# Graph and attention layer: one-hots compared with digits in PSUM, six tiles made in exchange gaps, histogram between parts of a projection, smaller table parts

## The reference

```python
def gnn(x, W, src, dst):                 # 6250 nodes of 256, 100000 edges
    h = x @ W
    mask = (src != dst)
    deg = segment_sum([mask, ones], [dst, loops])
    w = rsqrt(deg)[fsrc] * rsqrt(deg)[fdst] * [mask, ones]
    return segment_sum(w[:, None] * h[fdst], fsrc)
xn = layernorm(x)
x = x + gnn(xn, W, src, dst) + linear_attention(xn)      # 8 heads, elu + 1 features
x = x + top2_moe(layernorm(x))                           # 8 experts, 256 -> 1024 -> 256, gelu
```

## Time and profile before

| | us |
|---|---|
| median of 3 runs | 2474.34 (2472.77 to 2475.92) |
| the profiled execution's own time | 2474.63 |
| its span in the trace | 2472.7 |
| busy: PE, POOL, DVE, ACT | 2159.0, 1382.8, 1166.6, 1148.6 |
| first scatter, last scatter, first gather start at | 250.65, 448.89, 494.04 |

### The profile page before, as it was taken

How to read it: one execution, slowest core, us unless ns; L and a number is a source line. 1 busy time by engine, 2 the same in 40 slices (tenths; PEclk the granted TensorE clock), 3 DMA queues, 4 the chain that set the end, 5 groups by cost and what they waited for, 6 DMA issues and landing times.

```text
span 2472.7 us, 50507 instructions
## 1 busy us (share of the span) xinstructions
PE 2159.0 (87%) x11910; PEld 1729.7 (70%) x11911; DVE 1166.6 (47%) x2173; ACT 1148.6 (46%) x2813; POOL 1382.8 (56%) x1357
## 2 busy tenths in 40 slices
PE   2996897588889999999999887757999999999998
PEld 1664775366766666666666665426999999999997
DVE  8885653156665666656666565463222222222221
ACT  3664114266666666666666665652232323232322
POOL 3420787277777777777777776002454545444443
PEclk9998667799999999999999999957999999999999
DMA  4002000333333333333333337366666666666663
GB/s 147 1 9 43 3 4 3 119 104 104 105 105 105 106 104 105 105 105 105 104 106 104 105 105 101 109 207 195 186 175 187 175 186 178 183 181 180 183 178 79
DMA packets 136249, 289.74 MB, mean 117 GB/s; under 512 B 28580, under 2 KB 77920, under 8 KB 136067
## 3 DMA queue, kind: packets, MB, share of 16 engines
q0 software_dynamic: 67552, 137.24, 23.4%
q1 hardware_dynamic: 68643, 151.89, 19.0%
HBM read 251.51 MB, written 34.37 MB: 116 GB/s over the span
## 4 chain that ended last, share of the span: by engine, by line
PE 50%; POOL 13%; issue 11%; DVE 10%; DVEq 10%; DMA 3%; SPq 1%; ACT 0%; POOLq 0%; ACTq 0%
PE B L1584 15%; PE B L1593 15%; PE B L1480 13%; POOL BIG L507 7%; POOL edge_rows L496 6%; DVE ACC L553 4%; DVEq L884 3%; DVEq L713 2%; DVEq L876 2%; PE B L1553 2%; DMA BIG<-table,W2A 1%; DVE W2A L553 1%; PE B L1453 1%; DVE BIG L553 1%; PE B L1572 1%
## 5 line engine op out<-in xcount | busy, mean ns | idle before, releaser
L507 POOL DMA_INDIRECT BIG<-table,W2A x832 | 787.4, 946 | 297.4 <-issue 225.5
L553 DVE TENSOR_TENSOR ACC<-ACC,B 128x512 f32 x832 | 572.3, 688 | 403.5 <-PE B L1480 294.0
L1157 ACT ACTIVATE BIG<-B,SMALL 128x128 f32<-128x128 f32 (+1 forms) x889 | 251.1, 388 | 532.1 <-PE B L1584 532.0
L1480 PE MATMUL B<-BIG,W2A 128*128 128x256 f32 x1664 | 410.1, 390 | 75.7 <-DVE ACC L553 48.7
L1480 PE MATMUL B<-BIG 128*128 128x256 f32 x1664 | 406.2, 388 | 49.2 <-DMA BIG<-table,W2A 27.0
L1480 PEld LDWEIGHTS B<-BIG,W2A 128*128 128x128 f32 x1664 | 286.3, 189 | 176.3 <-issue 149.0
L1584 PEld LDWEIGHTS B<-BIG,W1A 128*128 128x128 f32 x3360 | 396.7, 194 | 6.7 <-DVE BIG L556 1.4
L1480 PEld LDWEIGHTS B<-BIG 128*128 128x128 f32 x1664 | 293.9, 190 | 153.2 <-issue 114.9
L1584 PE MATMUL B<-BIG,W1A 128*128 128x128 f32 x3360 | 397.4, 277 | 1.0 <-DVE BIG L556 1.0
L1593 PE MATMUL B<-W2A,BIG 128*128 x1680 | 380.1, 379 | 0.7 <-DVE BIG L553 0.7
L527 POOL DMA_INDIRECT out_dram<-BIG,SMALL x105 | 170.7, 1626 | 343.9 <-DVE BIG L556 343.9
(11 more groups left out here) (245 smaller groups left out, 2045.2 us busy)
## 6 DMA issues: line engine op xcount, KB each, us to landing
W1A<-in_w SPq DMA_DIRECT2D x105, 1024.0 KB
BIG<-table,W2A POOLq DMA_INDIRECT x832
W2A<-in_w SPq DMA_DIRECT2D x1, 8192.0 KB, 27.2
token_x<-BIG SPq DMA_DIRECT2D x24, 256.0 KB, 2.1
out_dram<-ACC SPq DMA_DIRECT2D x1, 6144.0 KB
W2A<-in_x SPq DMA_DIRECT2D x1, 3584.0 KB, 13.1
table<-ACC SPq DMA_DIRECT2D x2, 1792.0 KB, 10.2
W2A<-in_x SPq DMA_DIRECT2D x1, 2560.0 KB
```

What stands on the lines that cost most here:

```text
L507: pool.indirect_dma_start(G[h][:, u, :], None, table, bass.IndirectOffsetOnAxis(ap=dst_T[:, c:c + 1], axis=0)).then_inc(gath[h][u // 2], 16)
L553: return dve.tensor_tensor(o, a, b, op)
L1157: return nc.scalar.activation(o, i, fn, **kw)
L1480: last = mm(B[u][:, k * D:(k + 1) * D], OH[h % 2][:, u, k * P:(k + 1) * P], G[h][:, u, :], start=True, stop=True)
```

## The change

Seven edits, all in the preparation of the graph:

1. `digits` is no longer a bfloat16 array in SBUF. `iota` is copied once into PSUM bank B7, and `onehots` compares the digits in SBUF with that bank, spread over 16.
2. The one-hots of tiles 0 to 5 are made inside `compare_lanes`, one in each exchange gap, after `swap_ready` and ahead of the wait for the exchanged keys. Tile k there waits, as everywhere, for the histogram of tile k-2.
3. On PE those six histograms stand behind the projections 24, 28, 30, 34, 35 and 36. The other 43 stand, four to a projection, behind each of its four parts, in the projections 37 to 47. Projection 48 and then both `unpacked_columns` follow.
4. Half of the exchange transfers, and `raw3`, start from POOL instead of SP.
5. The wait for `counts_ready` and the product that follows it stand behind three projections instead of four, and the next such point behind four instead of six.
6. The table parts are 7, 14, 14, 11 and 3 tiles (before 14, 14, 12, 6 and 3), four ahead of the unpacking and the last behind its first four instructions.
7. ACT takes the root of the degrees behind projection 47 instead of 39.

```diff
-HT = 32
-HG = 8
-HIST_END = HT + NT // HG
-PARTS = ((0, 14), (14, 28), (28, 40), (40, 46), (46, NT))
+HT = 37
+HG = 4
+EARLY = (24, 28, 30, 34, 35, 36)
+HIST_END = HT + (NT - 1 - len(EARLY)) // HG
+PARTS = ((0, 7), (7, 21), (21, 35), (35, 46), (46, NT))
...
+            for k, apart in enumerate(SWAPS):
+                pool.wait_ge(swap_ready, k + 1)
+                for p in range(0, P, 2 * apart):
+                    pool.dma_start(swapped[p + apart:p + 2 * apart, :], keys[SWAP_FROM[k]][p:p + apart, :]).then_inc(swap_in_2, 16)
             pool.wait_ge(stage_ready, 1)
...
+            pool.wait_ge(scat, 16 * NROWS)
+            pool.dma_start(raw3, edge_rows[0:CPAD * RPC, :].rearrange("(j p a) r -> p j (a r)", p=P, a=RPC)).then_inc(raw_in, 16)
             pool.wait_ge(kv_done, NT)
...
-                tt(oh_lo[s], digits, lo, ALU.is_equal)
-                tt(oh_hi[s], digits[:, 0:NT, :], hi, ALU.is_equal).then_inc(oh_ready, 1)
+                digits = B[7][:, 0:P].unsqueeze(2)
+                tt(oh_lo[s], lo.to_broadcast([P, P, HB]), digits.to_broadcast([P, P, HB]), ALU.is_equal)
+                tt(oh_hi[s], hi.to_broadcast([P, NT, HB]), digits[:, 0:NT, :].to_broadcast([P, NT, HB]), ALU.is_equal).then_inc(oh_ready, 1)
...
                 dve.sem_inc(swap_ready, 1)
-                dve.wait_ge(swap_in, 16 * sum(P // a for a in SWAPS[0:k + 1]))
+                onehots(k, k % 2)
+                for there in (swap_in, swap_in_2):
+                    dve.wait_ge(there, 16 * sum(P // (2 * a) for a in SWAPS[0:k + 1]))
...
-            for t in range(4):
+            for t in range(3):
                 project(t, t % 2)
             pe.wait_ge(counts_ready, 1)
...
+            def project(t, s, degrees=()):
+                counts = iter(degrees)
                 keys_values(t, s)
+                count_next(counts)
                 features_queries(t, s)
+                count_next(counts)
                 if not isinstance(t, int) or t + 1 < NT:
                     transpose_x(t + 1, 1 - s)
+                count_next(counts)
                 sum_kv(t)
+                count_next(counts)
...
+            for t in range(EARLY[0] // 2 * 2, HT):
                 project(t, t % 2)
-                for k in range(HG):
-                    histogram((t - HT) * HG + k, k % 2)
-            project(HIST_END, HIST_END % 2)
-            histogram(NT - 1, 0)
+                if t in EARLY:
+                    histogram(EARLY.index(t), EARLY.index(t) % 2)
+            for t in range(HT, HIST_END + 1):
+                first = len(EARLY) + (t - HT) * HG
+                project(t, t % 2, range(first, min(first + HG, NT)))
```

More of the change, by code:

```diff
@@ L41 @@
 KEYS = 1024
+LB = LANES.bit_length() - 1
+FILLS = ROW // LANES
 RPC = P // ROW
@@ L78 @@
 SWAP_FROM = (1, 0, 1, 0, 1, 0)
[L79 to L80 removed]
+assert len(EARLY) == len(SWAPS) and HG == 4 and HIST_END < NT - 1 and CT_DVE % 7 == 0
+assert KEYS >= EC + FILLS * NGR and CPAD * RPC >= NROWS * P and 4 * P >= NBK * (RPC - 1)
 assert NGR <= 32 and UNROLL * 5 < 24
@@ L588, in _ @@
             ch.sync()
-            for k in range(3):
-                ch.add(ts(bit_I[:, k:k + 1], p_I, 4 + k, ALU.logical_shift_right, 1, ALU.bitwise_and))
+            for k in range(LB):
+                ch.add(ts(bit_I[:, k:k + 1], p_I, LISTS.bit_length() - 1 + k, ALU.logical_shift_right, 1, ALU.bitwise_and))
             ch.add(ts(list_ofI, list_ofI, LISTS - 1, ALU.bitwise_and))
             ch.sync()
-            for k, sg in enumerate((sg0, sg1, sg2)):
+            for k, sg in enumerate((sg0, sg1, sg2)[0:LB]):
                 ch.add(ts(sg, bit_I[:, k:k + 1], -2.0, ALU.mult, 1.0, ALU.add))
@@ L683, in _ @@
             dve.sem_inc(counts_ready, 1)
-            ch.add(ts(need[:, 0:NGR], need[:, 0:NGR], lane, ALU.is_gt))
+            for k in range(FILLS):
+                ch.add(ts(fill[:, NGR * k:NGR * (k + 1)], need[:, 0:NGR], -float(LANES * k), ALU.add, lane, ALU.is_gt))
             ch.add(ts(t0[:, 0:NGR], iota[:, 0:NGR], -1.0, ALU.mult, float(NGR), ALU.add))
-            ch.add(dve.memset(fill[:, NGR:KEYS - EC], float(NGR)))
+            ch.add(dve.memset(fill[:, FILLS * NGR:KEYS - EC], float(NGR)))
             ch.sync()
-            ch.link(tt(need[:, 0:NGR], need[:, 0:NGR], t0[:, 0:NGR], ALU.mult))
-            ch.link(ts(fill[:, 0:NGR], need[:, 0:NGR], -1.0, ALU.mult, float(NGR), ALU.add))
+            for k in range(FILLS):
+                ch.add(tt(fill[:, NGR * k:NGR * (k + 1)], fill[:, NGR * k:NGR * (k + 1)], t0[:, 0:NGR], ALU.mult))
+            ch.sync()
+            ch.link(ts(fill[:, 0:FILLS * NGR], fill[:, 0:FILLS * NGR], -1.0, ALU.mult, float(NGR), ALU.add))
             ch.link(ts(keysI[0][:, EC:KEYS], fill, float(GN * ((1 << CODE) + 1)), ALU.mult))
@@ L779, in _ @@
             dve.sem_inc(cgroup_ready, 1)
-            with dve.Fori(1, NT // 2) as i:
+            for t in range(len(EARLY), (len(EARLY) + 1) // 2 * 2):
+                onehots(t, t % 2)
+            with dve.Fori((len(EARLY) + 1) // 2, NT // 2) as i:
                 for s in range(2):
@@ L810, in scale_part @@
                 tt(a, a, dinv[:, first:last].unsqueeze(2).to_broadcast([P, last - first, D]), ALU.mult).then_inc(table_ready, 1)
-            for k in range(3):
+            for k in range(4):
                 scale_part(k)
@@ L1214, in _ @@
                 project(t, t)
-            with act.Fori(1, HIST_END // 2 + 1) as i:
+            with act.Fori(1, HIST_END // 2) as i:
                 for s in range(2):
                     project(i * 2 + s, s)
[L1218 to L1222, removed]
+            for t in range(HIST_END // 2 * 2, NT - 1):
+                project(t, t % 2)
+                if t == HIST_END:
+                    act.wait_ge(std_in, 2)
+                    cp(col[12][:, 0:NT], col[9][:, 0:NT], ACT.Sqrt).then_inc(std_out, 1)
             keys_values(NT - 1)
@@ L1416, in _ @@
             mm(B[6][:, 256:256 + NGR], same_list, col[0][:, 0:NGR], start=True, stop=True).then_inc(lists_ready, 1)
-            for t in range(4, 6):
-                project(t, t % 2)
+            project(3, 1)
             pe.wait_ge(counts_ready, 2)
```

34 lines of the change are left out of this document (14 added, 20 removed).

## The result

The changed kernel takes 2437.17 us (median of 4 runs, 2436.57 to 2440.18) beside 2474.97 us of the kernel before on the same chip: ratio 0.9853, 95% interval 0.9838 to 0.9867, 37.8 us less. The prediction had 28.5 us less, 2446, in a range of 2422 to 2465. The profiled execution's span is 2435.1 us (2472.7 before).

What follows compares the result with a forecast made beforehand. POOL's gathers were taken to set the pace, so only the first gather's start counts: PE's histogram end at 439 plus 26.5 gives 465.5 instead of 494.04, 28.5 us off 2474.63, hence 2446 us, range 2422 to 2465.

Steps and rivals of the forecast that it cites:

- The first gather sets the time: POOL sets the pace from the first gather on; its start moves from 494.04 to 465.5, ending the kernel 28.5 us earlier.
- Sort: DVE's sort starts 5.3 us earlier, waits for PE's histogram in the sixth gap, and ends at 265.1, 15.4 us later.
- Scatters: POOL's 128 scatters, unhindered by one-hots from PSUM, at 1.263 us a step, run from 266.0 to 430.1 (before 449.84).
- The step: A projection and four histograms on PE take 16 us, between 14.8 and 17.6, so the histogram is done at 439.
- From the degrees to the gather: From histogram end through root, table scaling, unpacking and POOL's wake-up to the first gather: 26.5 us.
- Which strand: Two strands meet at the first gather; PE's ends last, at 465.5 against the scatter's 447.
- PE's strand: Projections and histograms on PE until 439, then 26.5 us to the gather: lets it start at 465.5.
- the scatter's: Strand of sort, POOL's scatters, read of the rows (data at 439) and unpacking: lets the gather start at 447.
- The rival of a high clock: PE's clock stays high between pieces: step 12.8 to 13.5, scatter strand decides, 2420 to 2428 us; chance 0.25.

Runs made afterwards that it cites:

- d_sooner: Changed kernel with the six early histograms behind projections 24, 27, 28, 29, 33 and 35 instead of 24, 28, 30, 34, 35 and 36: 2425.49 us, 0.9805.
- c_uncut: Changed kernel with the four histograms of projections 37 to 47 behind the whole projection instead of between its parts: 2458.8 us, 0.9939.
- j_no_early: Changed kernel without the six early tiles, all 49 made behind the sort, from projection 34 on: 2434.55 us, 0.9841.
- h_five: d_sooner with five histograms to a projection instead of four: 2420.20 us, 0.9782.
- i_six: d_sooner with six histograms to a projection instead of four: 2422.73 us, 0.9789.
- b_sbuf_digits: Changed kernel with the one-hots' digits read from the float32 row in SBUF instead of its copy in PSUM: 2506.91 us, 1.0137.
- f_few_products: Changed kernel with only 4 of the 16 products of each one-hot tile on PE, so the degrees are wrong: 2427.42 us, 0.9813.
- n_few_psum: f_few_products with the degrees' roots copied into PSUM, from which the first four table parts are scaled: 2420.71 us, 0.9791.
- k_old_parts: Changed kernel with the table parts of the kernel before (14, 14, 12, 6 and 3 tiles): 2438.17 us, 0.9857.

## Why the prediction was right, and where it was off

- **The first gather sets the time**: right. 41.3 us there became 37.6 at the end.
- **Sort**: start 4.5 us earlier (5.3 in the sum), a tile 3.17 us (3.2), the sixth gap's wait until 245.61 (245.8), end at 264.4 (265.1). It was right that the early tiles make the sort 15 us later. But the sum had their worth in the filled pause of PE, and the run without them shows PE waiting hardly longer (9.34 us): without them the sort ends 24.5 us sooner.
- **Scatters**: 264.73 to 429.73 (266.0 to 430.1). One-hots from PSUM leave POOL alone; with digits in SBUF 72 us are lost beside the one-hots. The Trainium skill (SBUF — State Buffer, Who interferes with whom) says that a DVE instruction with two SBUF inputs contends with a GpSimd instruction that reads SBUF. The runs agree, for the one-hots and for the scaling: 2.72 to 3.50 us a scatter beside it, 0.96 with the roots in PSUM.
- **The step**, the term that was mis-sized: 16 in the sum, 14.5 measured, so the histogram ended at 422.90 and not at 439. The bound from the earlier trace rows, an uncut projection among histograms plus four histograms, 14.8, was the better value; my reason for going higher (pieces cut by histograms don't hold the clock) did not come true: the granted clock was 0.77, a mean between its two levels (1.2 and 2.4 GHz), higher than the 0.64 of 252.86 to 388.88 before. It went up and down, 1.00 from 280 to 292 and 0.50 from 294 to 302, and only the slowest steps took 16.1. The rule of the Trainium skill (TensorE: Matmul & The Clock Gate, HAM oscillation) is that bursts with pauses between begin slow. This trace bears it out in part: the clock did fall again and again, but for less than half of the time, and the step was 14.5 and not near 17.6.
- **From the degrees to the gather**: 26.5 us in the sum, 29.8 measured. The root took 0.37 us of waiting and not 2.3, but the read of the rows came at 442.42 instead of 439, past the 441 of its bound. The bound was for POOL's issue; what made it late was the table's writing beside it, which the sum did not see, because before the change the writing came after. The sum also put the table's last transfer at nothing, as fitting beside the rest. It does not fit: where the rows are early (d_sooner) the last part still lands 6.8 us behind its scaling, and the gather starts 28.5 us behind the histogram. So 2.0 of the 3.3 us are there with early rows as well, and 1.3 come with the late ones. With a step of 14.8 the sum would have given the measured 452.7, but by luck: the histogram would be 3.3 us too late and this stretch 3.3 too short.
- **Which strand**: the prediction let PE's strand end 18.5 us after the scatter's. In the five runs c_uncut, d_sooner, j_no_early, h_five and i_six, where the rows were early, the gather came 28.5 to 28.7 us behind the histogram's end; in b_sbuf_digits, f_few_products, n_few_psum and k_old_parts, where DVE waited longest for the rows, 13.2 to 13.7 behind the issue of their read. By these prices (an estimate) PE's strand, whose end is the table's writing, gives 451.5 for the changed kernel and the scatter's 447, and 452.7 came. So PE's was still the last, as predicted, but by 4 to 5 us only, and the wait of 2.90 for the rows cost about 1.3. Neither alone is worth much then: the read back on SP 0, because the writing stays; the histogram 28.6 us sooner 10 us, because then the scatters decide.
- **The rival of a high clock** gave 2420 to 2428; the run whose histogram ended at 394 reached 2427, and the one at a clock of 0.87 nothing, since the scaling then runs into the scatters. That hold stood in the earlier trace rows (the 4.33 us row), and the rival's price did not carry it.

Taken away one at a time, the digits in PSUM cost 70 us and the cut of the projection 21.6; the smaller parts and the early tiles as placed nothing that could be measured. Both of these taken away at once was not tried, and no run takes away the exchange transfers on POOL, the earlier start of the sort or the later root alone.

## What to carry to other kernels

Where several strands meet at one moment, price an edit by when each of the others ends: the edit without which the others lose gained nothing alone here. Where POOL-issued transfers lie on the last strand, a DVE instruction beside them is worth one input in PSUM even if it runs at half the speed (3.17 us a tile instead of 1.66 here), and that held for every such instruction that comes to lie beside them, the scaling too. To fill an engine's pause, move forward what needs nothing from the late strand, and put nothing there that holds that strand up: the same early tiles were worth 9 us or nothing, by where their histograms stood. And count the last transfers as a strand of their own: once the scaling was early, the writing of the table set the gather.

## What the hardware showed beyond that

- Plain transfers started by POOL cost its queue about 0.5 us each (four in 1.92 us), close to SP's 0.6 (four in 2.41 us), beside the scatters' 0.96.
- The same order of work ran at a granted clock of 0.74 in one profiled execution and of 0.87 in another over 269.32 to 390.00, with 7.6 us between the ends of the histogram; the two kernels differ only in table parts, which come later. Why is open.
